# Cross-attention and feed-forward of a Flamingo block: attention one head at a time over all 16 units, each head one tile of 128 tokens, the feed-forward of a tile between later heads, SiLU from Tanh

## Chip, cores and metric

One NeuronCore of one Trainium2 chip runs the whole kernel; the metric is device time in microseconds of that core.
The kernel before takes 286.89 us (median of three runs, 286.7 to 287.58). In what follows PE is TensorE, DVE is VectorE, ACT is ScalarE, POOL is GpSimd, SP is SyncE, whose queue only starts DMAs, and PEld is PE's weight load.

## What is computed

```
x: (16 units, 64 rows, 256)   ctx: (16, 64, 256)
q = layernorm(x);  k = v = ctx;  8 heads of 8 rows each, both axes of the scores are the 256 columns
qk  = einsum('bhdq,bhdl->bhql', q, k) / sqrt(8)
ret = einsum('bhql,bhdl->bhdq', softmax(qk), v)
x   = x + tanh(g_xattn) * gamma * ret
h   = silu(Wg @ quant8(layernorm(x))) * (Wu @ quant8(...))      weights rounded to -1, 0, 1
x   = x + tanh(g_ffn) * (Wd @ quant8(rms_norm(h)))              inner size 1024, 1024 tokens in all
```

So there are 128 attention problems (16 units by 8 heads), each with scores of 256 by 256, and then a quantised feed-forward over 1024 tokens, which is 8 tiles of 128.

## The kernel before

**Exact scores from bf16.** q and k are each split into three bf16 parts. The parts go to DRAM (`scr_q`, `scr_k`, `parts_to_dram`, L203) and come back stacked over 72 partitions (`load_stack`, L222 for q, L225 for k), so that one bf16 product of 72 rows gives the score in nearly full precision. Partitions 96 and 97 hold the negated row maximum in two parts, which `score` adds to the product.

**Attention, unit by unit.** A unit's eight heads stand side by side in one stack buffer (`qs`, `ks`, four buffers, a buffer is 2048 columns). Work goes in batches of four heads, two batches to a unit. For each head: `score_for_max` (L871, two matmuls of 256 columns into one of two banks `mb`), the row maximum on DVE (L663), and after a whole unit a transpose (L910), a copy on ACT (L522, `cast_maxima`), the low part on DVE (L671, `cut_maxima`), and two DMAs that write the maxima to the stack's shift rows (`shift_rows`, L254, `qs<-mp`). Then `score` (L884), Exp on ACT over two heads at once (L506), and the value product (L899, eight matmuls per two heads). The maxima run LEAD = 5 batches, 20 heads, ahead of the scores; the transpose of a unit's maxima stands eight heads ahead of its first score. `next_stack` reloads a buffer once all scores of its unit are done. The loop is rolled: first and last four units by hand, `Fori(1, ITERS - 1)` between.

**Sums.** The value product also gives the denominators. ACT copies them out (L514), POOL's queue sends them to DRAM and fetches them by token (L378, L387, L390), DVE inverts (L680, L682), SP sends the inverses round by DRAM (`scr_i<-inv` L270, `invt<-scr_i` L282), and POOL multiplies and adds to x (L405, L408).

**Feed-forward, after all attention.** DVE computes the statistics and quantises x for four tiles and then twice for two (L720 to L753). Per tile: PE transposes x (L954), eight matmuls of 512 columns for gate and up (L965, into two pairs of banks `s`), Silu on ACT (L576), the product on DVE (L778), the square sum on ACT (L586), the norm weight on POOL (L446), the maximum on DVE (L783), a few 128x1 scale steps on DVE (L791 to L799), scaling on POOL (L453), rounding on ACT (L597), eight transposes (L973), their copy on DVE (L804), the down product (L980), and the result (L811), which SP stores. Sixteen matmuls of `keep_warm` (L1000) stand near the beginning.

## Time and profile before

| | |
|---|---|
| median of the runs | 286.89 us (286.7, 287.58, 286.89) |
| profiled execution, first to last instruction | 285.5 us |
| PE busy | 166.9 us (58%) |
| DVE busy | 176.3 us (62%) |
| ACT busy | 127.1 us (45%) |
| POOL busy | 106.7 us (37%) |
| mean granted clock of TensorE | 0.875 |
| moved by DMA | 27.45 MB, mean 96 GB/s |

The span is what the profile covers; the run's time adds what lies around it, and for the profiled execution only the span is given (the runs lie 1.2 to 2.1 us above it). A busy share says how much an engine did and not whether it set the pace: no engine reaches two thirds here, so the pace is set by waits, and the chain of waits names them. Three stretches matter: the preparation to about 70 us (first maxima at 31 us, first scores at 71 us), attention to about 208 us, and the feed-forward to the end.

### The profile page before, as it was taken

The page shows a single profiled execution, that of the slowest core. Times are in us where ns is not written, and L with a number is a line of the kernel's source. Part 1 is how long each engine was busy: PE and PEld are TensorE (multiplying, and loading weights), DVE is VectorE, ACT ScalarE, POOL GpSimd, SP SyncE. Part 2 cuts the span into 40 slices and gives each one's busy share as a digit, 9 for nine tenths or more (in the row PEclk, how much of TensorE's full clock was granted, in tenths as well). Part 3 has the DMA queues.
Part 4 walks back from the last instruction along what each step waited for, and adds up shares of the span by engine and source line. Part 5 has one row for each costly group of instructions (what it writes and reads, how often), then busy time and mean ns, then how long its engine had stood idle before and what let it go on. Part 6 is the DMA issues. An engine that isn't in the chain of part 4 may idle for free.

```text
span 285.5 us, 4321 instructions
## 1 busy us (share of the span) xinstructions
PE 166.9 (58%) x1262; PEld 82.6 (29%) x1266; DVE 176.3 (62%) x349; ACT 127.1 (45%) x176; POOL 106.7 (37%) x177
## 2 busy tenths in 40 slices
PE   0000323400976856956948938939995686658564
PEld 0000000100633423523523514514542233234342
DVE  7898323500763743753744834825989987988962
ACT  1424000000682861743833824815687247447840
POOL 5928000001020330330350520341657877937960
PEclk9999999999997996995995996986999579678955
DMA  6666311991521921121222222231212200000011
GB/s 186 207 198 211 123 71 79 239 227 78 176 96 79 269 100 80 63 94 79 88 100 82 71 101 94 68 101 70 69 40 72 60 2 22 1 19 23 32 37 39
DMA packets 15494, 27.45 MB, mean 96 GB/s; under 512 B 4558, under 2 KB 8782, under 8 KB 15478
## 3 DMA queue, kind: packets, MB, share of 16 engines
q1 hardware_dynamic: 13430, 23.96, 26.0%
q0 software_dynamic: 2048, 3.29, 3.7%
q8 instruction: 8, 0.13, 0.2%
q14 instruction: 8, 0.07, 0.1%
HBM read 19.53 MB, written 7.47 MB: 95 GB/s over the span
## 4 chain that ended last, share of the span: by engine, by line
PE 28%; DMA 26%; DVE 18%; SPq 10%; issue 8%; POOL 7%; ACT 1%; POOLq 0%; DVEq 0%; ACTq 0%
DMA ks<-scr_k 15%; PE mb L871 8%; PE s L884 7%; PE ob L899 7%; DMA qs<-mp 6%; DMA scr_i<-inv 4%; SPq L222 3%; DVE qf L647 3%; POOL rk L446 3%; SPq L239 3%; PE s L965 2%; POOL qf L453 2%; DMA scr_q<-qp 2%; DVE kf L732 2%; SPq L225 1%
## 5 line engine op out<-in xcount | busy, mean ns | idle before, releaser
L663 DVE TENSOR_REDUCE mx<-mb 128x2 f32<-128x512 f32 x128 | 83.7, 687 | 88.1 <-PE mb L871 87.1
L871 PE MATMUL mb<-ks,qs 128*128 128x256 bf16 x256 | 58.9, 322 | 78.9 <-DMA ks<-scr_k 71.4
L506 ACT ACTIVATE pr<-s 128x1024 f32<-128x1024 f32 x64 | 64.5, 1020 | 26.3 <-PE s L884 25.9
L884 PE MATMUL s<-qs,ks 128*128 128x256 bf16 x256 | 54.5, 304 | 12.1 <-DMA qs<-mp 12.0
L369 POOL COPY vw<-vt 128x32 f32<-128x32 f32 (+1 forms) x64 | 10.7, 214 | 126.7 <-PE ob L899 84.7
L871 PEld LDWEIGHTS mb<-ks,qs 128*128 128x128 bf16 x256 | 21.7, 108 | 113.5 <-issue 63.8
L899 PE MATMUL ob<-pr,vw 128*32 128x256 f32 x512 | 44.4, 422 | 1.5 <-ACT osb L514 0.7
L522 ACT ACTIVATE mp<-mtb 16x128 bf16<-16x128 f32 x16 | 4.3, 266 | 79.5 <-PE mtb L910 53.4
L884 PEld LDWEIGHTS s<-qs,ks 128*128 128x128 bf16 x256 | 26.3, 108 | 22.7 <-DMA qs<-mp 13.3
L965 PE MATMUL s<-wt,xt 128*128 128x512 bf16 x60 | 21.1, 504 | 11.3 <-DVE rq L778 6.5
L446 POOL TENSOR_TENSOR rk<-rq,lnw 128x1024 f32<-128x1024 f32 x8 | 18.8, 2348 | 5.1 <-DVE rq L778 5.1
L576 ACT ACTIVATE sg<-s,gsc 128x512 f32<-128x512 f32 x16 | 10.8, 683 | 18.4 <-PE s L965 18.4
L899 PEld LDWEIGHTS ob<-pr,vw 128*32 128x32 f32 x512 | 10.8, 113 | 17.7 <-issue 13.9
L980 PE MATMUL mb<-wt,ht 128*128 128x256 bf16 x64 | 11.0, 330 | 7.7 <-DVE ht L804 7.7
L378 POOL DMA_DIRECT2D scr_o<-osb x16 | 10.4, 648 | 9.3 <-ACT osb L514 6.2
L965 PEld LDWEIGHTS s<-wt,xt 128*128 128x128 bf16 x64 | 7.1, 119 | 21.9 <-issue 8.6
L597 ACT ACTIVATE yi<-qf 128x1024 bf16<-128x1024 f32 x8 | 8.4, 1055 | 6.2 <-POOL qf L453 6.0
L778 DVE TENSOR_TENSOR rq<-s,sg 128x512 f32<-128x512 f32 x16 | 10.3, 682 | 0.5 <-ACT sg L576 0.5
L387 POOL DMA_DIRECT2D num<-scr_o x16 | 9.9, 616 | 2.0 <-issue 1.7
L647 DVE TENSOR_SCALAR qf<-qf,mv,rs 128x256 f32<-128x256 f32 x8 | 9.4, 1232 | 1.8 <-POOL rs L341 1.8
L783 DVE TENSOR_REDUCE ym<-rk 128x1 f32<-128x1024 f32 x8 | 9.7, 1210 | 0.2 <-POOL rk L446 0.2
L980 PEld LDWEIGHTS mb<-wt,ht 128*128 128x128 bf16 x64 | 6.6, 114 | 10.9 <-DVE ht L804 9.4
(84 smaller groups left out, 205.2 us busy)
## 6 DMA issues: line engine op xcount, KB each, us to landing
qs<-scr_q SPq DMA_DIRECT2D x15, 288.0 KB
ks<-scr_k SPq DMA_DIRECT2D x15, 288.0 KB
scr_k<-kp SPq DMA_DIRECT2D x10, 256.0 KB, 2.9
scr_o<-osb POOLq DMA_DIRECT2D x16, 128.0 KB, 3.0
scr_q<-qp SPq DMA_DIRECT2D x6, 256.0 KB, 3.4
qf<-in_xh SPq DMA_DIRECT2D x2, 512.0 KB, 5.5
kf<-in_kh SPq DMA_DIRECT2D x2, 512.0 KB, 6.9
vt<-in_vt SPq DMA_DIRECT2D x1, 1024.0 KB, 27.8
```

What stands on the lines that cost most here:

```text
L369: nc.gpsimd.tensor_copy(dst, src).then_inc(v_filled, 1)
L378: pool.dma_start(scr_o[bass.ds(i * BUFS + k, 1)].rearrange("o p n -> (o p) n"), osb[:, k % 2, :]).then_inc(sums_out[k % 2], DMA)
L446: nc.gpsimd.tensor_tensor(y[:, par, :], z[:, par, :, :].rearrange("p a n -> p (a n)"), lnw[:, :], ALU.mult).then_inc(y_done, 1)
L506: nc.scalar.activation(pr[:, slot:slot + 2, :, :].rearrange("p h c n -> p h (c n)"), s2[pair][:, :, :], ACT.Exp, scale=float(DH) ** -0.5). ...
L576: nc.scalar.activation(sg[:, h, :], s2[h][:, 0, :], ACT.Silu, scale=gsc[:, bass.ds(t, 1)]).then_inc(silued, 1)
L647: nc.vector.tensor_scalar(cols, cols, mv[:, j, 0:1], rs[:, j:j + 1], ALU.subtract, ALU.mult).then_inc(normed, 1)
L663: nc.vector.tensor_reduce(mx[:, unit % 2, 2 * j:2 * j + 2], mb[h % 2][:, :].rearrange("p (c n) -> p c n", c=KC), axis=AX.X, op=ALU.max, ne ...
L871: mm = nc.tensor.matmul(mb[h % 2][:, c * COLS:(c + 1) * COLS], columns(qs, b, j, c), head(ks, b, j), start=True, stop=True)
L884: mm = nc.tensor.matmul(s2[pair][:, h % 2, c * COLS:(c + 1) * COLS], columns(ks, b, j, c), head(qs, b, j), start=True, stop=True)
L899: mm = nc.tensor.matmul(ob[32 * g:32 * g + 32, r, :], vw[:, r, c, 4 * a + g, :], pr[:, 4 * (b % 2) + g, c, :], start=(a == 0 and c == 0), ...
L965: mm = nc.tensor.matmul(s2[h][:, n, :], xt[:, c, :], w[:, c, h * 512:(h + 1) * 512], start=(c == 0), stop=(c == KC - 1))
L980: mm = nc.tensor.matmul(op_, ht[:, c, :], wdt[:, c, :], start=(c == 0), stop=(c == IC - 1))
```

## The change

The order of the work is new on every engine. Attention now runs head by head: head t of all 16 units is one stack (4096 columns, three buffers), and its 128 output rows (16 units by 8 rows) are exactly one tile of the feed-forward. The program is unrolled into 208 steps; step n is (T, p) with T = n // 16 and p = n % 16. In a step stand: the maximum product of problem n, the score of problem n - 14 (LAG), every fourth step the values of four problems, and at fixed p the feed-forward of tile T - 4 or T - 5. Scores go to a ring of three single banks that the transposed maxima share; Exp is now per head. The maxima of eight problems form a group (at both ends of the order of four), and its transpose stands five steps ahead of the group's first score. Attention ends in T = 8, the feed-forward in T = 12. Gate and up have one bank each (`gb`, `ub`), which the transposes and the down product use too.

Silu(x) comes from Tanh: ACT computes tanh(x/2), DVE adds 1 and multiplies by x, then by the up product (two DVE operations where one was). The 128x1 scale steps, the normalisation of x and the cutting of the weights move from DVE to POOL (more than a dozen small operations per tile, each waiting for the one before); the copy of `ht` and the last rounding of x move from DVE to ACT. POOL's DMAs of the sums move to SP. `keep_warm`, the zero rows and the separate load of x by token are gone. Preparation: head 0's parts are made and stored first, then the rest; the parts go out as runs of 512 bytes, and the loads of a stack have other outer dimensions.

The core of the diff:

```diff
...
@@ -20,23 +10,57 @@
...
-IC = INNER // P
-BUFS = 4
+KC, IC = COLS // P, INNER // P
+PER = UNITS
+TOTAL = TILES * PER
+SPAN = UNITS * COLS
...
 QMAX = 127.0
 ROUND = 1.5 * 2.0 ** 23
-SHIFT_ROW = 96
 TWO_ONES = 1.0 + 0x3F80 / 2.0 ** 23
-LEAD = 5
-ITERS = UNITS // BUFS
+KROWS = 9 * DH
+SROWS = KROWS + 2
 DMA = 16
-FREE = 2
-FREE1 = 1
-ANY = -99
+STACKS = 3
+VBUFS = 4
+
+LAG = 14
...
-            def load_stack(unit, k, lo, n_cols, arrived):
-
-                src = scr_q[bass.ds(unit, 1), :, :, lo:lo + n_cols].rearrange("o n d c -> (o n d) c")
-                sp.dma_start(qs[0:9 * DH, k, lo:lo + n_cols],
-                             bass.AP(src.tensor, src.offset, [[0, 3], [FREE_N, 3 * DH], [1, n_cols]])).then_inc(arrived, DMA)
-                src = scr_k[bass.ds(unit, 1), :, :, lo:lo + n_cols].rearrange("o n d c -> (o n d) c")
-                sp.dma_start(ks[0:9 * DH, k, lo:lo + n_cols],
-                             bass.AP(src.tensor, src.offset, [[DH * FREE_N, 3], [FREE_N, 3 * DH], [1, n_cols]])).then_inc(arrived, DMA)
-
-            parts_to_dram(parts, 0)
-            parts_to_dram(parts[:2], 1)
-            sp.wait_ge(q_clear, 1)
-            sp.wait_ge(k_clear, 1)
-            sp.wait_ge(parts_out[0], 8 * DMA)
...
-            def next_stack(i, k):
-
-                sp.wait_ge(scored, i * 16 + 4 * (k + 1))
-                sp.sem_inc(passed[3], 1)
-                sp.dma_start(qs[SHIFT_ROW:SHIFT_ROW + 2, k, :], zrow[:, :]).then_inc(stack_in[k], DMA)
-                load_stack(i * BUFS + (k + BUFS), k, 0, FREE_N, stack_in[k])
-
-            def shift_rows(i, k):
-
-                buf = k % BUFS
-                sp.wait_ge(max_cut, i * BUFS + (k + 1))
-                for n in range(2):
-                    row = qs[SHIFT_ROW + n:SHIFT_ROW + n + 1, buf, :].rearrange("o (h q) -> o h q", q=P)
-                    sp.dma_start(row, mp[:, n, :]).then_inc(shift_in[buf], DMA)
...
+            def load_stack(t, lo, hi, arrived):
+                src = scr_q[t].rearrange("a d u c -> (a d) (u c)")[:, lo:hi]
+                sp.dma_start(qs[0:KROWS, t % STACKS, lo:hi], bass.AP(src.tensor, src.offset, [
+                    [SPAN, 3 * DH], [0, 3], [1, hi - lo]])).then_inc(arrived, DMA)
+                for r in range(3):
+                    src = scr_k[t, r:r + 3].rearrange("a d u c -> (a d) (u c)")[:, lo:hi]
+                    sp.dma_start(ks[r:KROWS:3, t % STACKS, lo:hi], src).then_inc(arrived, DMA)
+
+            def wait_parts(t):
+                sp.wait_ge(q_out[t], DMA)
+                sp.wait_ge(k_out[t], 2 * DMA)
+
+            def next_stack(t):
+                wait_parts(t)
+                sp.wait_ge(k_ones, min(t, STACKS - 1) + 1)
+                if t >= STACKS:
+                    sp.wait_ge(scored, PER * (t - STACKS + 1))
+                load_stack(t, 0, SPAN, stack_in[t % STACKS])
...
+            for T in range(1, 13):
+                if 0 <= T - 2 < TILES:
+                    sums_to_dram(T - 2, 1)
+                if 1 < T + 1 < TILES:
+                    next_stack(T + 1)
+                if T < TILES + 1:
+                    shift_rows(2 * T if T < TILES else groups - 2)
+                if T == TILES:
+                    shift_rows(groups - 1)
+                if 0 <= T - 2 < TILES:
+                    sums_by_token(T - 2)
+                    inv_to_dram(T - 2)
+                if T < TILES:
+                    shift_rows(2 * T + 1)
+                if 0 <= T - 1 < TILES:
+                    sums_to_dram(T - 1, 0)
+                if 0 <= T - 2 < TILES:
+                    inv_by_token(T - 2)
+                if 0 <= T - 5 < TILES:
+                    store(T - 5)
             for par in range(2):
-                sp.wait_ge(o_out[par], (TILES // 2 + 1) * DMA)
-
+                sp.wait_ge(o_out[par], DMA * TILES // 2)
 
         @block.gpsimd
         def _(pool):
-            pool.sem_inc(att_done, FREE)
...
-            def silu(t, first):
-                for h in range(2):
-                    act.wait_ge(gu_done, t * 2 + (h + 1))
-                    if not first:
-                        act.wait_ge(z_done, t * 2 + (h - 1))
-                    act.sem_inc(passed[1], 1)
-                    nc.scalar.activation(sg[:, h, :], s2[h][:, 0, :], ACT.Silu,
-                                         scale=gsc[:, bass.ds(t, 1)]).then_inc(silued, 1)
-
-            def square(t, par, first):
-                act.wait_ge(z_done, t * 2 + 2)
...
+            def tanh_gate(t, h):
+
+                act.wait_ge(gu_done, 2 * t + h + 1)
+                act.wait_ge(a_scaled, t + 1)
+                if t >= 1:
+                    act.wait_ge(z_done, 2 * (t - 1) + h + 1)
+                nc.scalar.activation(th[:, h, :], gb[:, :], ACT.Tanh, scale=ghs[:, t:t + 1]).then_inc(tanh_done, 1)
+
...
+            def exp(m):
+
+                b = m // 4
+                if m % 4 == 0 and b >= 2:
+                    act.wait_ge(pv_done, b - 1)
+                act.wait_ge(scored, m + 1)
+                nc.scalar.activation(pr[:, b % 2, m % 4, :], score_slot(m)[:, :], ACT.Exp, scale=float(DH) ** -0.5).then_inc(exp_done, 1)
+
...
-            def gate_up(t, par, first):
-
-                for h in range(2):
-                    dve.wait_ge(silued, t * 2 + (h + 1))
-                    if not first and h == 0:
-                        dve.wait_ge(squared, t - 1)
-                        dve.wait_ge(y_done, t - 1)
-                    nc.vector.tensor_tensor(z[:, par, h, :], s2[h][:, 1, :], sg[:, h, :], ALU.mult).then_inc(z_done, 1)
-
-            def max_h(t, par):
+                nc.vector.tensor_scalar(wgh[:, :], wmean[:, 0:1], 0.5, None, ALU.mult).then_inc(w_stat, 1)
...
+            def gate_up(t, h):
+
+                dve.wait_ge(tanh_done, 2 * t + h + 1)
+                nc.vector.scalar_tensor_tensor(out=th[:, h, :], in0=th[:, h, :], scalar=1.0, in1=gb[:, :],
+                                               op0=ALU.add, op1=ALU.mult).then_inc(z_half, 1)
+                dve.wait_ge(z_half, 2 * t + h + 1)
+                if t >= 2 and h == 0:
+                    dve.wait_ge(squared, t - 1)
+                    dve.wait_ge(y_done, t - 1)
+                nc.vector.tensor_tensor(z[:, t % 2, h * 512:(h + 1) * 512], ub[:, :], th[:, h, :], ALU.mult).then_inc(z_done, 1)
+
+            def max_y(t):
...
+            for n in range(STEPS):
+                T, p = divmod(n, PER)
+                if n < TOTAL:
+                    reduce(n)
+                if n - 2 in TURN_AT:
+                    cut_maxima(TURN_AT[n - 2])
+                if T == 2 and p == 3:
+                    weigh_means()
+                if p == 2 and 0 <= T - 3 < TILES:
+                    mean_x(T - 3)
+                if p == 3 and 0 <= T - 3 < TILES:
+                    var_x(T - 3)
+                if p == 4 and 0 <= T - 4 < TILES:
+                    gate_up(T - 4, 0)
+                if p == 6 and 0 <= T - 3 < TILES:
+                    max_x(T - 3)
+                if p == 7 and 0 <= T - 4 < TILES:
+                    gate_up(T - 4, 1)
+                if p == 8 and 0 <= T - 2 < TILES:
+                    invert(T - 2)
+                if p == 12 and 0 <= T - 4 < TILES:
+                    max_y(T - 4)
+                if p == 13 and 0 <= T - 5 < TILES:
+                    result(T - 5)
 
         @block.tensor
         def _(pe):
-            pe.sem_inc(pv_done, FREE)
-            pe.sem_inc(h_turned, FREE1)
-            pe.sem_inc(down_done, FREE1)
-
...
+            def ring_free(who):
+
+                i = SLOT[who] - 3
+                if i >= 0:
+                    kind, at = RING[i]
+                    if kind == "score":
+                        pe.wait_ge(exp_done, at + 1)
+                    else:
+                        pe.wait_ge(max_cut, at + 1)
+
+            def score_for_max(n):
...
-            def keep_warm(count):
-
-                for n in range(count):
-                    nc.tensor.matmul(ob[:, :, :].rearrange("p r n -> p (r n)"), identb[:, :], wt[:, 0, 0:512], start=True, stop=True)
-
-            period(0, 0, 0, TILES)
-            keep_warm(16)
...
+            for n in range(STEPS):
+                T, p = divmod(n, PER)
+                if n < TOTAL:
+                    score_for_max(n)
+                if n in TURN_AT:
+                    turn_maxima(TURN_AT[n])
+                if 0 <= n - LAG < TOTAL:
+                    score(n - LAG)
+                b = (n - PV_LAG) // 4
+                if (n - PV_LAG) % 4 == 0 and 0 <= b < TOTAL // 4:
+                    values(b)
+                if T == 2 and p == 2:
+                    pe.wait_ge(consts, 3)
+                    sum_weights()
+                if p == 2 and 0 <= T - 4 < TILES:
+                    gate_up(T - 4, 0)
+                if p == 5 and 0 <= T - 4 < TILES:
+                    gate_up(T - 4, 1)
+                if p == 9 and 0 <= T - 5 < TILES:
+                    turn_h(T - 5)
+                if p == 11 and 0 <= T - 5 < TILES:
+                    down(T - 5)
+                if p == 12 and 0 <= T - 3 < TILES:
+                    turn_x(T - 3)
 
```

On SP's queue, in the rolled loop of the kernel before, one unit (`scored` counts scores done, `max_cut` the low parts of maxima):

```order
L245 DMA qs<-zrow 2x2048 [waits scored]
L222 ISA
L222 DMA qs<-scr_q 72x1x2048
L225 ISA
L225 DMA ks<-scr_k 72x1x2048
L251 REGISTER_ALU
L254 DMA qs<-mp 1x16x128 [waits max_cut]
L254 DMA qs<-mp 1x16x128
```

The same queue after the change, one whole T (16 heads) of the attention:

```order
L257 DMA scr_o<-osb 128x256 [waits o_copied]
L223 DMA qs<-scr_q 72x1x4096 [waits k_ones,scored,k_out4,q_out4]
L227 DMA ks<-scr_k 24x4096 x3
L249 DMA qs<-mp 1x16x128 [waits max_cut]
L249 DMA qs<-mp 1x16x128
L265 DMA den<-scr_o 128x1x32 [waits sums_out1]
L267 DMA num<-scr_o 128x1x256
L272 DMA scr_i<-inv 8x16x32 [waits inverted]
L249 DMA qs<-mp 1x16x128 [waits max_cut]
L249 DMA qs<-mp 1x16x128
L257 DMA scr_o<-osb 128x256 [waits o_copied]
L279 DMA invt<-scr_i 128x1x256 [waits inv_out1]
```

One reload now brings 16 heads instead of 8, as four DMAs instead of two; the shift rows of a group still stand behind the reload, and the sums' DMAs now stand in the same queue.

PE's queue after the change, p = 2 to p = 7 of a T with feed-forward (`sr_n` are the ring's banks, `gb` and `ub` gate and up):

```order
L810 MATMUL sr<-qs,ks 128x256 [waits max_cut]
L810 MATMUL sr<-qs,ks 128x256
L824 MATMUL ob<-pr,vw 32x256 [waits o_copied,v_filled,exp_done]
L824 MATMUL ob<-pr,vw 32x256 x7
...
L858 MATMUL gb<-wt,xt 128x512 [waits z_done]
L858 MATMUL gb<-wt,xt 128x512
L858 MATMUL ub<-wt,xt 128x512 x2
L791 MATMUL mb<-ks,qs 128x256 [waits max_taken]
L791 MATMUL mb<-ks,qs 128x256
L810 MATMUL sr<-qs,ks 128x256 [waits exp_done,shift_in0]
```

The second score behind a transpose now waits for `max_cut`, because the ring has three banks; the second half of gate and up waits for DVE's product of the first (`z_done`); and the next maximum products stand behind both.

## Rows read from the trace of the kernel before

**Rows 1.** The page: busy tenths of DVE and of the DMA engines, in 40 slices.
```profile
DVE  7898323500763743753744834825989987988962
...
DMA  6666311991521921121222222231212200000011
```
**Rows 2.** Chain of waits: start us, us, what.
```profile
36.23 0.71 SPq L225
...
42.61 7.57 SPq L239
...
50.23 2.57 SPq L254
...
52.84 17.89 DMA qs<-mp
...
120.58 10.03 DMA ks<-scr_k
...
148.32 10.21 DMA scr_i<-inv
```
**Rows 3.** Waits: engine, line, releaser: us in total, times, longest us.
```profile
DVE mx L663 <- PE mb L871: 87.1, 60, 12.3
```
**Rows 4.** Stretches: length, busy PE, PEld, DVE, ACT, POOL, clock, DMA share, GB/s.
```profile
50.00:62.00 12.00, 4.14 (x14) 0.87 (x13) 4.64 (x8) 0.00 (x0) 0.00 (x0) 1.00 0.97 247
...
126.50:139.50 13.00, 8.77 (x66) 4.32 (x67) 5.46 (x9) 5.10 (x7) 2.10 (x7) 0.74 0.24 91
138.00:144.00 6.00, 5.98 (x65) 3.40 (x63) 5.17 (x12) 5.12 (x8) 2.16 (x7) 1.00 0.21 71
```
**Rows 5.** Shift DMAs (L254) issued at 182.83 and 183.48: us from issue to landing.
```profile
DMA to landing us min/median/max: 2.2/5.5/8.9
```
**Rows 6.** Chain, PE in attention: half clock at 134, full clock at 138.
```profile
132.83 1.01 PE ob L899 x8
...
134.38 0.43 PE s L884 x2
...
138.89 0.57 PE ob L899 x8
139.46 0.33 PE mb L871 x2
139.79 0.22 PE s L884 x2
```
**Rows 7.** Groups by line: out<-in, shapes, count | busy us, mean ns | idle before.
```profile
L663 DVE TENSOR_REDUCE mx<-mb 128x2 f32<-128x512 f32 x128 | 83.7, 687 | 88.1 <-PE mb L871 87.1
L506 ACT ACTIVATE pr<-s 128x1024 f32<-128x1024 f32 x64 | 64.5, 1020 | 26.3 <-PE s L884 25.9
L576 ACT ACTIVATE sg<-s,gsc 128x512 f32<-128x512 f32 x16 | 10.8, 683 | 18.4 <-PE s L965 18.4
L446 POOL TENSOR_TENSOR rk<-rq,lnw 128x1024 f32<-128x1024 f32 x8 | 18.8, 2348 | 5.1 <-DVE rq L778 5.1
L439 POOL TENSOR_TENSOR rh<-vh,mhalf 128x1 f32<-128x1 f32 x8 | 4.4, 552 | 5.1 <-ACT vh L591 4.3 <-POOL qf L453 0.8
L453 POOL TENSOR_SCALAR qf<-rk,sh 128x1024 f32<-128x1024 f32 x8 | 9.0, 1121 | 2.0 <-DVE sh L799 1.9 <-issue 0.2
L527 ACT ACTIVATE wt<-wf 128x2048 bf16<-128x2048 f32 x3 | 5.7, 1912 | 0.0
L783 DVE TENSOR_REDUCE ym<-rk 128x1 f32<-128x1024 f32 x8 | 9.7, 1210 | 0.2 <-POOL rk L446 0.2
```
**Rows 8.** Timeline of the feed-forward: start us, us, engine, line, operation.
```profile
246.64 3.59 PE L965 MATMUL s<-wt,xt 128*128 128x512 bf16 x8 [1.14 <-DVE rq L778]
...
261.14 1.89 PE L965 MATMUL s<-wt,xt 128*128 128x512 bf16 x8
...
275.35 1.03 PE L973 MATMUL mtb<-identb,yi 128*128 128x128 bf16 x8 [0.49 <-ACT yi L597]
277.17 1.89 PE L980 MATMUL mb<-wt,ht 128*128 128x256 bf16 x8 [0.79 <-DVE ht L804]
```

1180 lines of the change are left out of this document (518 added, 662 removed).

## The prediction

> **What bounds the kernel now.** I read the page first, then the chain of waits, then single stretches. No engine is full, and DVE, the busiest, has two holes, near 60 us and in a saw-tooth through attention [rows 1]. The waits say whose fault that is: DVE stands 87.1 us for the maximum products on PE [rows 3], and the chain goes from those to `ks<-scr_k`, a stack reload of 10.0 us that comes once per unit [rows 2]. In a stretch where almost only such reloads run, the DMA share is 0.21 at 71 GB/s, while the loads of 50 to 62 us reach 0.97 and 247 GB/s [rows 4]. 0.21 of 16 engines is three: the reload of a unit (288 KB for q and 288 KB for k) sits on three engines, whose outer dimension in `load_stack` is 3. Eight heads then cost 10 us, 16 heads 20.5 us, whatever the engines do.
>
> The Trainium skill, DMA: Bandwidth & Descriptors, "Why a DMA increments its semaphore by 16 and not by 1", gives the rule: a DMA uses the largest number of engines up to 16 that divides the outermost dimension of both sides. By that rule the old reload has 3 engines, and the trace agrees (0.21); the new ones, 24 rows against 72 and 24 against 24, would have 12.
>
> Where the reload does not hold it, PE does: in full clock two heads take 0.57 for the values and 0.33 and three times 0.22 for the products, with gaps 1.55 us, where DVE needs 2 times 0.69 [rows 6, 7]. In half clock the same is 2.84 us (value product 1.01, each pair 0.43) [rows 6]. The preparation ends at 70.7 us, when the first shift rows land after 17.9 us behind stacks and weights [rows 2]. The feed-forward needs 77 us from 208 us on.
>
> **Preparation.** Head 0 alone is loaded, split and stored, so I put its stack in place at 22 us instead of 31 (0.25 MB instead of 2 MB in front of the first statistics, casts of 256 columns, a 3 us round to DRAM, four issues of 0.7 us [rows 2]). 14 maxima follow at 0.66 us each, and PE then stands at score 0. What it waits for is a long queue: SP issues 14 DMAs of parts (9 us, to 32), then `vt` (landed near 39), POOL fills the values and only then sets the one rows of the other stack buffers (42), SP reloads stack 1 (to 45), and the first shift rows land at 49.5. Score 4 at n = 18 needs the second group, whose shift rows stand behind 3 MB of weights: at 247 GB/s [rows 4] that is 12.7 us from 47 on, so with landing **62 us**. The step that is late before (17.9 us behind the same weights) is thus late again; the gain is 9 us, with 18 maxima done instead of 20.
>
> **A T without feed-forward.** The reload of 1.18 MB takes 4.2 us if 12 engines each keep the rate of rows 4's three (24 GB/s), 6.4 us at the 15.4 GB/s that each of 16 has at 247 GB/s; both are below a T, so the 20.5 us bound goes. What is late next is the shift row. It stands behind the reload in every ring: before, one issued right behind a reload lands after 8.9 us, otherwise after 2.2 [rows 5]. Before, it has eight heads of time, now five. I count from the start of a T: copy of the sums and its DMA to 2.2, four reload issues to 5.3, shift issue to 6.5, landing at 8.7. PE reaches p = 6 at 5.5 (DVE's six maxima 4.1, the low part 0.27, and 1.4 in which DVE has no bank because PE waits for the low part at p = 3 and then does the values). Wait 3.2 us. From p = 6 to p = 13 the same takes 7.2; the second group is not behind a reload and costs 0.8; two steps and values 2.1. Sum 5.5 + 3.2 + 7.2 + 0.8 + 2.1 = 18.8, say **19 us**, for T = 3. T = 1 and T = 2 also carry the weights on ACT: 16 Exp of 0.60 (half of 1.02 and a fixed part), three passes of 2.1 [rows 7], 0.9 of copies, 17 us, in segments that wait for the same shift rows: 15.5 us from n = 18 to the end of T = 1 and **20.5 us** for T = 2.
>
> **A T with feed-forward (four of them).** DVE: 16 x 0.687 = 11.0, low parts 0.54, four operations of 512 columns 2.7 (the two of the SiLU cost 1.4 more than before), `ym` 1.2, statistics, `am`, inverse and result 1.8: 17.3 us. ACT: Exp 9.6, tanh 1.4, square 1.25, `yi` 1.06, `ht` 1.05, copies 2.0: 16.3 us. PE in full clock: 12.4 for attention, 1.9 for gate and up [rows 8], 0.6, 1.1 and 0.3 for the rest: 16.3 us. POOL: 2.35 + 1.12 + 0.55 for each of five powers [rows 7], ten small operations at 0.2 to 0.4, which no row shows alone and which I take at 0.3 with their waits, two additions of 0.9: 13 us. None of these is the period, because they wait for each other: tanh of half 0 stands behind the score that waits for the low part, gate and up of half 1 behind DVE's product of half 0, tanh of half 1 behind the score that waits for the shift row (landed at 8.7, needed at 8.6, so here nearly free), and the down product with the values at p = 11 leaves DVE without a bank for 2.8 us. Followed step by step in full clock: 8.7 to p = 6, 13.1 from there, **21.8 us**. In half clock PE needs twice as long. A stretch of 13 us behind such a wait has a granted clock of 0.74 [rows 4], which is 6.8 us at 1.2 GHz and the rest at 2.4; I take 1.2 us a T for it: **23 us**, and 92 us for the four.
>
> **The rest.** T = 8 has the last scores and no maxima; ACT sets the pace with 15.5 us, I take 17. From T = 9 the feed-forward is alone with one pair of banks: gate and up 1.0, tanh 0.75, two DVE operations 1.35, the same again, eight transposes 0.9, `ht` 1.05, down 1.9 [rows 8], next transposes and copy 0.8: 10.1 with 0.1 for each hand-over, and POOL's own chain of scales is 11: 12 us each for T = 9 and 10. From T = 11: product of half 1 at 6.5, POOL's weight 2.35, maximum 1.2, scales and scaling 2.75, `yi` 1.05, transposes 1.03, copy 1.05, down 1.89, result 0.5, store 2: **21 us**, 45 us in all.
>
> **Sum**: 62 + 15.5 + 20.5 + 19 + 92 + 17 + 45 = 271 us, against the profiled span of 285.5. The median stands 1.4 above that span, so the time is **272.4 us**. In short: 9 us from the start, attention with half of the feed-forward in it ends about 18 us later than attention before, and after it 45 to 62 us are left instead of 77.
>
> **Rivals.**
> *Tight pipeline.* The waits I added (low part, values without a bank, shift row) overlap better, and a T costs what its fullest engine does plus a little: 17, 17 and 15 for T = 1 to 3, 19 for the next four. 62 + 14 + 17 + 15 + 76 + 15 + 44 + 1.4 = 244. For it: before, DVE idles only 0.26 in 1.55 us in full clock. Against: the order has more waits in a line than before. Chance 0.22.
> *Half clock holds (slower).* The order has two or three short stops of PE per T where before there is one long one per 20 us. If half clock covers most of it, attention costs 16 heads x 1.42 = 22.7 us of PE [rows 6], plus 3.59 for gate and up [rows 8] and 2 for the rest: 28.3 us in T = 4 to 7, 22 in T = 2 and 3. 62 + 17 + 44 + 113 + 18 + 46 + 1.4 = 301. It decides from about 26.5 us per T on. For it: the clock of 0.74 behind one stop [rows 4]. The Trainium skill, TensorE: Matmul & The Clock Gate, "HAM oscillation", says that waits for DMA put the clock back again and again, which speaks for this. Chance 0.15.
> *Reload still on three engines (slower).* 1.18 MB at 71 GB/s are 16.6 us, the shift row behind it lands at 19 us of a T, which becomes 29 us or more: over 330 us. Chance 0.04.
> *Small operations on POOL set the pace (slower).* At 0.5 us each instead of 0.3, and with DVE's and the DMAs' hand-overs, POOL needs 16 us, and the way of the inverse round by DRAM (10.2 us before, behind a reload [rows 2]) pushes `yi` onto ACT's queue ahead of the Exp: 26.5 us a T and 15 in the end, 294. Chance 0.09.
>
> **How the numbers follow.** The forecast has 0.50. Its own range, 258 to 286, comes from the POOL and `vt` chain (5 us either way), the 1.2 us of clock (0 to 3 per T), and 1 us per T of overlap. Taking in the tight pipeline's 244 to about half and both slower cases up to 297 leaves 2 in 10 outside: 247 to 297. A measurement of this kernel tells 0.3%, 0.9 us, from no change. Faster: nearly all of 0.50, and 0.22: 0.71. The same: 0.04. Slower: 0.25.
>
> **What would show it.** Right: first maximum product at 22 us, a stop of PE from 31 to 50 and another to 62, DMA share above 0.5 in a reload, a wait of PE for `qs<-mp` of 3 us per T early on, maxima of T = 4 starting near 117 and its period near 23 us, PE's last attention product near 225. Wrong: reloads at a share of 0.2, granted clock below 0.75 on average in attention, or POOL as the releaser of DVE's `am` and ACT's `yi` in each T.

## The result, and the profile after

| | before | after |
|---|---|---|
| median | 287.54 us (286.7 to 288.25, 6 runs) | 311.73 us (304.93 to 316.44, 6 runs) |
| ratio | | 1.066, 95% interval 1.058 to 1.074 |
| profiled span | 285.5 us | 314.5 us |
| PE, DVE, ACT, POOL busy | 166.9, 176.3, 127.1, 106.7 us | 191.6, 142.3, 138.1, 150.2 us |
| mean granted clock | 0.875 | 0.751 |

The change makes the kernel slower by 6.6%; the forecast was 272.4 us (247 to 297), faster. The changed kernel scatters by 11 us where the kernel before scatters by 1.5 (and by up to 5 in the later sets). Its profiled execution is the longest of the six. The ratio comes from the two shortest runs, which span 302.8 and 305.3 us at a clock of 0.787 and 0.779, and single stretches of this profile can be some microseconds longer than in those.

The page: rows of the 40 slices, and two of the groups.

```profile
PE   0045004378877956866897888488877675344433
DVE  3775202254433553474554745555584433334320
PEclk9999999996557576796555677857897999555555
DMA  3679739920240060151106013401101112000000
...
L675 DVE TENSOR_REDUCE mx<-mb 128x2 f32<-128x512 f32 x128 | 85.4, 684 | 112.4 <-PE mb L791 110.8
L810 PE MATMUL sr<-qs,ks 74*128 74x256 bf16 x256 | 63.7, 344 | 54.4 <-DMA qs<-mp 36.2 <-DVE mp L682 17.1 <-ACT pr L522 1.2
```

Against [rows 1, 3] three things stand out. DVE did the same 128 maxima at the same price, and waited for PE not 87.1 but 110.8 us. The DMA row now has short peaks with nothing between them. And the clock row lies at 5 to 7 in most slices of attention; its mean is 0.751, where before it was 0.875.

One caution on that row. It shows 1.00 up to its first recorded change, at 65.7 us here and near 74 us before, although the matmuls up to there have the durations of half clock (a score pair takes 0.61 to 0.64 us, and 0.38 to 0.39 in full clock). So the means are too high in both kernels, and where a clock matters, the duration of a matmul has to confirm it.

The reload itself did what was forecast. Windows of the kernel after, in a reload and over the blocks T = 2 to T = 8 and the rest; columns as in [rows 4].

```profile
113.00:118.00 5.00, 2.88 (x22) 1.42 (x14) 2.40 (x4) 1.39 (x3) 2.23 (x4) 0.54 0.76 207
...
82.80:109.90 27.10, 21.55 (x132) 10.48 (x131) 11.63 (x23) 15.63 (x23) 13.98 (x10) 0.56 0.23 66
109.90:134.60 24.70, 17.52 (x136) 8.93 (x135) 11.69 (x23) 10.41 (x23) 7.01 (x14) 0.72 0.26 72
134.60:162.70 28.10, 21.84 (x140) 10.77 (x139) 15.73 (x28) 12.45 (x26) 11.16 (x21) 0.67 0.23 63
162.70:192.40 29.70, 25.51 (x160) 12.68 (x159) 16.02 (x29) 14.32 (x29) 13.88 (x25) 0.62 0.24 65
192.40:222.60 30.20, 22.79 (x156) 12.01 (x155) 15.93 (x29) 14.29 (x28) 12.15 (x23) 0.72 0.25 63
222.60:247.30 24.70, 17.90 (x157) 9.52 (x156) 15.04 (x29) 14.44 (x31) 12.99 (x24) 0.93 0.10 30
247.30:262.80 15.50, 11.22 (x117) 5.67 (x115) 6.02 (x12) 12.28 (x24) 8.87 (x16) 1.00 0.17 46
262.80:314.50 51.70, 21.05 (x91) 9.91 (x88) 15.20 (x24) 16.91 (x24) 30.95 (x56) 0.54 0.06 19
```

A share of 0.76 in the reload is twelve engines of sixteen, where [rows 4] had 0.21, three. Its data moves from about 112 to 119 us, somewhat longer than the forecast's 4.2 to 6.4 us. The forecast's rule for the number of engines (the Trainium skill, DMA: Bandwidth & Descriptors, "Why a DMA increments its semaphore by 16 and not by 1") therefore agrees with the trace.

Then the blocks. Each T = 4 to 7 was to take 23 us; they take 28.1, 29.7, 30.2 and 24.7. In each of them PE is busy for most of the time (21.8, 25.5, 22.8, 17.9 us) at a clock of 0.67, 0.62, 0.72 and 0.93, for work that in full clock is 16 us. The one with the least PE time is T = 7, the block in which no stack is reloaded.

Where PE stops, its timeline shows at T = 3, which begins at 109.9 (start, duration, and in brackets the idle time ahead and what ended it).

```profile
112.17 0.39 PE L810 MATMUL sr<-qs,ks 74*128 74x256 bf16 x2 [1.46 <-DVE mp L682]
112.49 1.14 PE L824 MATMUL ob<-pr,vw 128*32 128x256 f32 x16
113.56 0.61 PE L791 MATMUL mb<-ks,qs 72*128 72x256 bf16 x2
...
120.13 0.61 PE L810 MATMUL sr<-qs,ks 74*128 74x256 bf16 x2 [4.26 <-DMA qs<-mp]
120.53 0.63 PE L791 MATMUL mb<-ks,qs 72*128 72x256 bf16 x2
120.96 0.64 PE L810 MATMUL sr<-qs,ks 74*128 74x256 bf16 x2
121.52 1.94 PE L824 MATMUL ob<-pr,vw 128*32 128x256 f32 x16
...
126.90 0.54 PE L810 MATMUL sr<-qs,ks 74*128 74x256 bf16 x2 [0.98 <-DVE mp L682]
127.37 1.93 PE L824 MATMUL ob<-pr,vw 128*32 128x256 f32 x16
...
132.06 1.07 PE L824 MATMUL ob<-pr,vw 128*32 128x256 f32 x16
```

There are three stops of 1.46, 4.26 and 0.98 us, and between and behind them the same sixteen value matmuls take 1.94 us in half clock and 1.07 in full. SP issued those shift rows at 113.56, behind the four transfers of the reload:

```profile
109.90 0.32 SPq L257 DMA_DIRECT2D scr_o<-osb  x1
110.40 0.84 SPq L223 DMA_DIRECT2D qs<-scr_q  x1
111.28 2.23 SPq L227 DMA_DIRECT2D ks<-scr_k  x3
113.56 1.19 SPq L249 DMA_DIRECT2D qs<-mp  x2
114.80 0.65 SPq L265 DMA_DIRECT2D den<-scr_o  x1
```

They were usable at 120.1, 10.2 us into the block (forecast: 8.7). The DMA engines are busy with the reload until about 119 us: the share is 0.57 from 118 to 118.5 us and 0.07 from 119 to 119.5.

### The profile page after: what moved, and what is told of

Same layout as the page of the kernel before. It is cut to its first block, busy times and chain, and to the rows that moved or that the text cites. A ratio compares the mean times of both kernels' runs of the same rounds, so it can differ in the third digit from the quotient of the medians.

```text
span 314.5 us, 3742 instructions
## 1 busy us (share of the span) xinstructions
PE 191.6 (61%) x1252; PEld 94.5 (30%) x1252; DVE 142.3 (45%) x257; ACT 138.1 (44%) x247; POOL 150.2 (48%) x236
## 4 chain that ended last, share of the span: by engine, by line
PE 34%; POOL 16%; DMA 16%; DVE 13%; SPq 9%; issue 5%; ACT 5%; POOLq 0%; ACTq 0%; DVEq 0%
PE ob L824 12%; DMA qs<-mp 11%; PE sr L810 8%; PE mb L791 7%; DVE mx L675 6%; SPq L227 3%; POOL qf L373 3%; PE ub L876 2%; DMA xh<-in_xh 2%; SPq L253 2%; PE gb L858 2%; DMA invt<-scr_i 2%; DVE wf L720 2%; PE ub L858 2%; POOL scr_q L385 2%
## 5 line engine op out<-in xcount | busy, mean ns | idle before, releaser
L675 DVE TENSOR_REDUCE mx<-mb 128x2 f32<-128x512 f32 x128 | 85.4, 684 | 112.4 <-PE mb L791 110.8
L522 ACT ACTIVATE pr<-sr 128x512 f32<-128x512 f32 x128 | 75.3, 594 | 119.2 <-PE sr L810 118.7
L810 PE MATMUL sr<-qs,ks 74*128 74x256 bf16 x256 | 63.7, 344 | 54.4 <-DMA qs<-mp 36.2
L791 PE MATMUL mb<-ks,qs 72*128 72x256 bf16 x256 | 66.9, 357 | 28.0 <-DMA ks<-scr_k 19.2
L810 PEld LDWEIGHTS sr<-qs,ks 74*128 74x128 bf16 x256 | 28.1, 120 | 72.8 <-DMA qs<-mp 38.9
L791 PEld LDWEIGHTS mb<-ks,qs 72*128 72x128 bf16 x256 | 25.9, 121 | 62.9 <-issue 37.3
L446 POOL TENSOR_TENSOR wf<-wf,lnw 128x1024 f32<-128x1024 f32 x8 | 18.8, 2350 | 12.1 <-DVE wf L726 8.1
L858 PE MATMUL gb<-wt,xt 128*128 128x512 bf16 x32 | 12.2, 471 | 15.2 <-DVE wf L726 13.0
L876 PE MATMUL ub<-wt,ht 128*128 128x256 bf16 x64 | 13.9, 392 | 5.5 <-ACT ht L590 5.5
L720 DVE SCALAR_TENSOR_TENSOR wf<-wf,gb 128x512 f32<-128x512 f32 x16 | 10.9, 683 | 12.3 <-ACT wf L569 12.1
L867 PE MATMUL gb<-identb,yi 128*128 128x128 bf16 x64 | 7.0, 275 | 14.9 <-DVE wf L726 11.1
L858 PE MATMUL ub<-wt,xt 128*128 128x512 bf16 x32 | 12.3, 474 | 0.0
```

Source lines behind the costliest of these rows:

```text
L446: nc.gpsimd.tensor_tensor(y[:, t % 2, :], z[:, t % 2, :], lnw[:, :], ALU.mult).then_inc(y_done, 1)
L522: nc.scalar.activation(pr[:, b % 2, m % 4, :], score_slot(m)[:, :], ACT.Exp, scale=float(DH) ** -0.5).then_inc(exp_done, 1)
L675: nc.vector.tensor_reduce(mx[:, h % 2, 2 * at:2 * at + 2], mb[n % 2][:, :].rearrange("p (c n) -> p c n", c=KC), axis=AX.X, op=ALU.max, neg ...
L720: nc.vector.scalar_tensor_tensor(out=th[:, h, :], in0=th[:, h, :], scalar=1.0, in1=gb[:, :], op0=ALU.add, op1=ALU.mult).then_inc(z_half, 1)
L791: mm = nc.tensor.matmul(mb[n % 2][:, c * COLS:(c + 1) * COLS], qs[0:KROWS, t % STACKS, at:at + P], ks[0:KROWS, t % STACKS, u * COLS:(u + 1 ...
L810: mm = nc.tensor.matmul(score_slot(m)[:, c * COLS:(c + 1) * COLS], ks[0:SROWS, t % STACKS, at:at + P], qs[0:SROWS, t % STACKS, u * COLS:(u ...
```

## Experiments

Theory at the start: the new order stops PE two or three times a block, at the low part and at the shift rows behind the reload, and the rest of the loss is what these stops bring with them. Rivals: half clock by itself, the second operation of the SiLU on DVE, the value product that leaves DVE without a bank, and POOL. Each set of runs had the kernel before beside it; its median moved by less than 2 us between sets. Where a ratio to it was formed, the ratio decides; medians of the changed kernel carry its scatter of 11 us.

**One part alone: the reload on twelve engines in the kernel before.**

```diff
-  bass.AP(src.tensor, src.offset, [[0, 3], [FREE_N, 3 * DH], [1, n_cols]])
+  bass.AP(src.tensor, src.offset, [[FREE_N, 3 * DH], [0, 3], [1, n_cols]])
...
-  sp.dma_start(ks[0:9 * DH, k, ...], AP([[DH * FREE_N, 3], [FREE_N, 3 * DH], ...]))
+  for r in range(3):
+      sp.dma_start(ks[r:9 * DH:3, k, ...], scr_k[unit, r:r + 3, ...])
```

> The kernel before with one part of the change alone: a stack is reloaded with 24 as outer dimension (one DMA for q, three for k) instead of 3. Theory (reload bound): attention before is held by the three DMA engines at 10 us a unit; with more engines a reload takes 4 to 6 us, 16 heads cost 13 to 15 us of PE instead of 20.5, and the run is 25 to 40 us shorter, near 250 to 262 us. Rival (the wait only moves): shift rows and issues on the queue (two more DMAs of 0.7 us per unit) take its place, gain under 10 us. If the reload still has three engines: DMA share stays 0.2 and the time stays at 287 us.

230.39 us (229.09 to 230.88), ratio 0.806 (0.799 to 0.812), 56 us less. Its page:

```profile
PE   0000033739999599979977999999389458487573
DVE  6998743738887588768866897889998979979942
PEclk9999999999999999999999999999857997889855
DMA  5857654699638823443533443212110000001101
```

The last row maximum starts at 149 us instead of 207 and the last value product at 161 instead of 218. PE is at 9 tenths in most slices of attention, the clock stays full in them, and the 60 us from 80 to 140 hold 68 of the maxima, which is 14 us for 16 heads. So the old bound was worth 56 us, more than the 25 to 40 expected, and the kernel before with that one edit is some 80 us faster than the changed kernel, which has the edit too (75 by the ratios).

**The reload undone in the changed kernel.**

```diff
-  [SPAN, 3 * DH], [0, 3], [1, hi - lo]])
+  [0, 3], [SPAN, 3 * DH], [1, hi - lo]])
...
-  for r in range(3):
-      src = scr_k[t, r:r + 3] ...
-      sp.dma_start(ks[r:KROWS:3, ...], src)
+  sp.dma_start(ks[0:KROWS, ...], AP([DH * SPAN, 3], [SPAN, 3 * DH], ...))
```

> The changed kernel with its reload undone: the rows of a stack are fetched with an outer dimension of 3 as before, on three DMA engines. Theory (the reload's engines are the one good part of the change; in the kernel before they were worth 56 us): a reload takes 10 us again, each stop for the shift rows behind it grows by 4 to 6 us, 325 to 345 us. Rival (the waits for the low part and the shift rows hide a long reload, since a whole stack lies between its issue and its use): 308 to 318 us.

380.15 us (379.76 to 381.84), ratio 1.325 (1.316 to 1.334): 68 us more than the changed kernel, above the range of either theory. A window behind the issue of a reload, and the block T = 4:

```profile
156.00:170.00 14.00, 1.43 (x7) 0.70 (x5) 2.16 (x4) 1.19 (x2) 2.28 (x7) 0.50 0.21 83
...
183.70:217.60 33.90, 18.09 (x141) 9.04 (x140) 15.37 (x28) 12.30 (x27) 11.13 (x21) 0.75 0.15 52
```

The share is 0.21 again, and PE is all but idle in the first window: the shift rows behind the long reload stop it (109.9 us in 8 stops by the waits). T = 3 to 6 take 32 to 34 us, T = 7, without a reload, 24.2. So the reload's engines were not one small part. What the rest of the change costs can be read twice: 92 us on three engines (380 against 288), and some 80 us on twelve (312 against 230).

**The shift rows ahead of the reload**, in the changed kernel.

```diff
+  if T < TILES + 1:
+      shift_rows(2 * T if T < TILES else groups - 2)
   if 1 < T + 1 < TILES:
       next_stack(T + 1)
-  if T < TILES + 1:
-      shift_rows(2 * T if T < TILES else groups - 2)
```

> The changed kernel with the shift rows of group 2T issued before the reload of stack T+1, and not behind it. Theory of my prediction: PE waits about 3 us per T for them in T = 2 and 3 and less than 1 us later; so 5 to 9 us less in all. Theory of the clock: the stop of 3 us is one of those that put the clock back, and the T after it get shorter as well, 10 to 15 us less. Rival: the waits for the low part and for banks are the ones that count, under 3 us.

298.57 us (297.86 to 300.44), ratio 1.045 (1.036 to 1.054): 13.2 us less in the median, 6 us by the ratios (1.045 against 1.066). The first number lies in the range of the theory of the clock, the second in that of the prediction's theory, so the times don't decide between them. The blocks speak for the clock: T = 4 to 7 take 100.2 us instead of 112.7, with PE idle for 24.8 us where it was 24.7, and busy for 75.4 where it was 88.0. The wait of PE for `qs<-mp` went from 36.2 us in 7 stops to 23.0 in 2, and those two are in the preparation.

**Fillers in the stops, on the changed kernel.** Matmuls into the free bank, behind the last maximum: 4 at p = 3 and 11, 6 at p = 5, 6 and 14 of T = 3 to 7, 8 to 40 in the end.

> The changed kernel with filler matmuls of 256 columns (results overwritten) where PE stands: in T = 3 to 7 four before a score that waits for the low part, six before one that waits for shift rows and before the second half of gate and up; after attention 8 to 12 before each feed-forward step. Theory of the clock: half clock is what makes a T of feed-forward 28 us and not 22; with the stops filled the granted clock in T = 3 to 8 goes from 0.7 to above 0.9, those T shrink by 4 to 6 us each, the tail from T = 9 by 5 us, in all 20 to 30 us less, 280 us. Rival (waits in a line set the period): clock rises but the time stays within 5 us, or gets longer by the fillers (about 0.1 us each, some 3 us per T).

303.79 us (302.82 to 307.34), ratio 1.066 (1.056 to 1.076). The clock rose from 0.751 to 0.898, and the result is about the changed kernel's shortest run. T = 5 and 6 in full clock:

```profile
161.10:185.50 24.40, 19.89 (x186) 11.74 (x185) 15.81 (x29) 14.20 (x29) 10.18 (x20) 1.00 0.29 78
185.50:210.80 25.30, 19.66 (x184) 11.53 (x183) 15.71 (x29) 14.02 (x29) 12.83 (x24) 1.00 0.28 76
```

They take 5 us less than in the changed kernel's profile, T = 4 (clock 0.70) and T = 7 nothing less. But these fillers don't make the kernel fast: PE is busy for 19.9 and 19.7 us in these two blocks where its own work is 16, so some 4 us of each are now fillers. The scatter is 4.5 us; whether the clock makes the 11 us of the changed kernel isn't shown, for of its six runs the one with the highest mean clock, 0.797, took 313.3 us.

**Values in two pieces, on the changed kernel**, so that DVE has a bank sooner: 8 matmuls one step earlier, 8 one step later.

> The changed kernel with the value products of four heads in two pieces of eight matmuls, two steps apart (one step earlier and one later), as the kernel before had them. Theory of coupling (DVE is left without a bank for the 1.9 us that the values take in half clock, more with the down product behind it): 1 to 2 us less per T, 8 to 14 us in all. Theory of the clock alone: no stop of PE goes away, within 3 us. Rival: the copy of the sums on ACT at the start of a T now comes one step later, slower by 1 to 4 us.

316.94 us (315.02 to 323.1), ratio 1.104 (1.093 to 1.115). A miss: slower, and by more than the rival allowed. DVE still waits 107.4 us for the maximum products (110.8 before), so the split doesn't take that wait away. The clock row has a mean of 0.842 here, but up to 144 us it holds no recorded change and shows 1.00, and the matmuls say otherwise (eight value matmuls inside that stretch and in full clock later):

```profile
112.87 1.08 PE L825 MATMUL ob<-pr,vw 128*32 128x256 f32 x8
...
173.90 0.64 PE L825 MATMUL ob<-pr,vw 128*32 128x256 f32 x8
```

PE ran at half clock through T = 2 and T = 3, which take 27.0 and 27.7 us, and is busy for 206.3 us in all, against 191.6. So this run doesn't speak against half clock as a cause. Why it stayed there for so long isn't shown.

**Without the product of x in the SiLU, on the changed kernel.** This kernel leaves out the operation that forms (1 + tanh) times x; the gate is tanh alone, 16 DVE operations fewer.

> The changed kernel with one of the two DVE operations of the SiLU left out (the product of 1 + tanh with x: the gate is then tanh alone), 16 operations of 0.68 us. Theory (they stand in the line z of half 0, gate and up of half 1, tanh, z of half 1, also in the tail): 1.4 us less per T in nine T, 10 to 14 us. Rival (they are covered by waits for PE): under 4 us.

307.64 us (306.18 to 310.3), ratio 1.070 (1.062 to 1.079). No effect by the ratio: the extra operation of the SiLU costs nothing that shows here.

**The cut of the maxima one step earlier**, on top of the shift rows first.

```diff
-  if n - 1 in TURN_AT:
-      cast_maxima(TURN_AT[n - 1])
+  if n in TURN_AT:
+      cast_maxima(TURN_AT[n])
...
-  if n - 2 in TURN_AT:
-      cut_maxima(TURN_AT[n - 2])
+  if n - 1 in TURN_AT:
+      cut_maxima(TURN_AT[n - 1])
```

> The changed kernel with the shift rows ahead of the reload (as in a1_shift_first) and, besides, the maxima of a group cast one step earlier on ACT (before that step's Exp) and their low part one step earlier on DVE. Theory (waits in a line set the period): PE waits 1 to 1.5 us for the low part twice a T and the shift rows leave one step earlier; 1.5 to 2.5 us less per T, 10 to 18 us below a1_shift_first's 298.6. Rival (clock): the stops stay, only shorter, so the clock stays near 0.8 and the gain is under 5 us.

281.99 us (281.38 to 287.38), ratio 0.982 (0.972 to 0.991): 16.6 us less than with the shift rows first alone, by moving two small operations, as the theory had it. The clock is in it as well (mean 0.835 against 0.800): T = 4 to 7 are 11.1 us shorter, and PE's busy time makes 5.4 of that, its idle time 5.7. PE's wait for the low part fell from 15.5 to 3.5 us. Since the shift rows went first, another wait has come up in the list of waits (10.4 us in 4 stops there, not in the changed kernel's list), and here it is the next to go (us in all, times, the longest):

```profile
DVE inv L690 <- DMA den<-scr_o: 14.0, 5, 4.9
```

DVE's inverse waits for the sums, whose fetch is queued on SP behind the reload, as the shift rows were.

**The same cut, with the shift rows left behind the reload.**

> The changed kernel with the early cast and cut of the maxima alone; the shift rows stay behind the reload, where they waited 36.2 us in 7 stops. Theory (waits in a line on PE's queue: each takes away its own time whatever the others do): 293 to 300 us, as much less than 311.7 as the same edit gave behind the other order (16.6 us). Rival (the shift rows behind the reload end the second stop of each block whenever the cut comes, so half of the gain is hidden): 301 to 308 us.

303.65 us (295.51 to 308.27), 8.1 us less than the changed kernel; no ratio was formed, so the medians have to do. T = 4 to 6 fall from 28.1, 29.7, 30.2 to 27.3, 26.6, 27.2 us, T = 7, which has no reload to wait for, from 24.7 to 20.4 at full clock. By the median that is the rival, but the shortest run, 295.51 us, lies in the theory's range, so the times alone don't decide. The waits do: those of PE for the low part fell from 17.1 to 4.6 us, and those for shift rows rose from 36.2 to 41.9. Of 12.5 us won at the low part, 5.7 are waited for at the shift rows instead.

**Fillers on top of the shift rows first**, fewer than above.

> a1_shift_first with fillers in the stops of attention only, from T = 1 on (three before a score that waits for the low part, four before one that waits for shift rows and before the second half of gate and up). Theory of the clock: granted clock in attention above 0.95, T = 2 to 7 shorter by 2 to 3 us each, 12 to 18 us below 298.6. Rival (waits in a line): the T shrink by less than 1 us each.

302.19 us (299.61 to 304.98), ratio 1.049 (1.037 to 1.061), against 1.045 without them. No gain, but no test of the clock either: its mean rose only from 0.800 to 0.822, and T = 4 to 7 lie at 0.74 to 0.93, where above 0.95 was expected.

**A longer lag**, the scores 18 instead of 14 behind the maxima, on the changed kernel, with the shift rows first and the sums later to suit.

> The changed kernel with LAG 18 instead of 14, so that a group's maxima are turned nine steps ahead of its first score and not five, shift rows ahead of the reload, and the steps that hang on the sums four steps later. Theory (lead too short): no wait of PE for shift rows is left in T = 1 to 7, 3 to 4 us less per T than in the changed kernel; 285 to 293 us. Rival: the later sums hold up the feed-forward of the next T, or the waits for the low part and the banks take over: 298 us as in a1_shift_first, or more.

293.94 us (291.27 to 301.37), ratio 1.017 (1.007 to 1.027). The shift rows cost PE 3.0 us in one stop, but the low part, which stands at a fixed distance from its transpose, still 16.7 in 14, and the preparation has a second wait for a stack, 17 us. Lag cures the transfer in the blocks, not the cut.

**The sums' fetch ahead of the reload**, on top of the early cut.

```diff
+  if 0 <= T - 2 < TILES:
+      sums_by_token(T - 2)
   if 1 < T + 1 < TILES:
       next_stack(T + 1)
```

> The version with the stack's shift rows ahead of the reload and the early cut (281.99 us), with the fetch of the softmax sums issued ahead of the next stack's reload on SP too. Theory (the sums' fetch stood behind the reload, DVE waited 14.0 us in 5 stops for it and PE behind DVE): DVE's wait for den falls below 3 us, T=3 to T=7 are 1 to 3 us shorter each, 270 to 276 us. Rival (the reload, issued later, now comes late for the next stack, or PE was waiting for something else at the same time): 280 to 284 us, with a wait of PE for the stack in its place.

269.9 us (267.12 to 274.12; before in the same set 288.01), 12.1 us less; no ratio was formed, but all its runs lie below all those without the edit. The wait for `den` is gone from the list of waits. Its blocks T = 3 to T = 8 and the rest:

```profile
95.60:114.80 19.20, 15.47 (x132) 7.77 (x131) 11.44 (x23) 10.26 (x24) 7.45 (x16) 0.84 0.34 92
114.80:136.70 21.90, 18.18 (x143) 9.71 (x143) 15.14 (x28) 12.63 (x28) 9.71 (x18) 0.83 0.32 81
136.70:156.40 19.70, 16.06 (x157) 9.32 (x157) 15.43 (x29) 14.03 (x29) 12.75 (x23) 1.00 0.36 97
156.40:177.40 21.00, 17.61 (x158) 9.82 (x157) 15.55 (x29) 14.15 (x29) 13.07 (x25) 0.92 0.34 91
177.40:198.00 20.60, 15.91 (x154) 8.97 (x154) 14.60 (x28) 14.22 (x31) 12.63 (x23) 1.00 0.12 35
198.00:214.20 16.20, 12.35 (x114) 6.26 (x115) 6.54 (x13) 12.21 (x24) 11.71 (x22) 0.89 0.15 44
214.20:265.50 51.30, 20.71 (x90) 9.89 (x89) 15.20 (x24) 16.93 (x24) 30.11 (x54) 0.54 0.07 19
```

T = 4 to 7 now take 83.2 us instead of 112.7. PE's busy time in them fell from 88.0 to 67.8 us, for the same matmuls, and its idle time from 24.7 to 15.4. So two thirds of what the three edits gave in these blocks is the clock, which came back by itself when the stops went. That isn't only the long profile of the changed kernel: the kernel without the product of x, profiled in 308.3 us and otherwise with the same matmuls, takes 109.1 us for T = 4 to 7 with PE busy for 86.7. The reload, now issued 3.7 to 5.2 us into a block instead of 0.5, is not late.

**Fillers on this version.**

> The fastest version of the changed kernel (269.9 us, mean clock 0.853) with filler matmuls in the stops of T=3 to T=7 and of the tail. Theory (with the waits gone TensorE's own work ends the blocks, so the clock counts: 86 us at half clock): mean clock over 0.92 and 260 to 266 us. Rival (the blocks are still chains through ACT and DVE, and the fillers fill time that comes back as nothing, as in the changed kernel itself): 268 to 274 us.

273.15 us (269.63 to 274.11), ratio 0.954 (0.949 to 0.958), clock 0.958. The clock is where the theory put it, the time is the rival's. T = 5 and 6 take 23.5 and 23.2 us with PE busy 20.7 and 20.5, where without fillers it is 16.1 and 17.6: they hold PE by more than the clock gives. The experiment doesn't tell what a full clock would be worth for free.

**The scale steps back on DVE for all tiles**, five of six small operations ahead of each hidden row's quantization.

> The same version, with five of the six 128x1 scale steps ahead of each hidden row's quantization moved from GpSimd back to VectorE, the inverse root computed on GpSimd right after the weighing. Theory (the last four tiles are a chain through GpSimd, some 12 us a tile, of which these small steps are 1.9 us of work and more in handovers): the tail of about 51 us is 5 to 10 us shorter, so 5 to 10 us below the version above. Rival (the tail is a chain of handovers whoever computes the steps, or VectorE's new waits hold its maxima in T=4 to T=7): within 2 us of it or slower.

278.63 us (275.21 to 279.42), ratio 0.971 (0.964 to 0.977), 8.7 us slower. T = 9 to the end takes 48.7 us instead of 51.3, but T = 4 to 7 take 98.1 instead of 83.2. Of these 14.9 us, 10.5 are PE's busy time, at a clock of 0.81 where it was 0.93, and DVE waits 28.3 us for the maximum products where it was 19.7. The list of waits has none of DVE for POOL's scales in these blocks, so that the new steps hold the maxima, as the rival says, isn't shown directly.

**The same for the last four tiles alone.**

> The same fastest version with the small scale steps on VectorE for the last four tiles alone. Theory (the tail is a chain through GpSimd and these steps are in it, while VectorE has nothing else to do there): 3 to 6 us less, 264 to 267 us, T=1 to T=7 unchanged. Rival (the tail's length is set by the handovers): 269 to 272 us.

264.99 us (259.84 to 275.58, 6 runs), ratio 0.924 (0.919 to 0.929). The end falls to 47.4 us, and T = 6 to 8 are unchanged to 0.2 us. Ahead of T = 8 the two kernels do the same, and yet T = 3 begins 3.5 us earlier and is 2.3 us shorter at a higher clock (0.90 for 0.84), T = 4 is 1.0 us shorter, and T = 5 took 22.5 us at a clock of 0.88 where it took 19.7 at 1.00. Blocks that differ like that are the likely reason why these runs lie 16 us apart. This is the fastest form of the changed order that I found, and 35 us slower than the kernel before with the reload edit.

**The preparation of the fastest kernel reordered**: in the kernel before with its reload on twelve engines, the first shift rows after two stacks, the value table and the third stack behind them, the weights last.

> The kernel before with its reload on twelve engines (230.39 us), and in the prologue the first stack's shift rows issued after two stacks instead of after three and the value table, the value weights after the second stack's shift rows. Theory (the first scores at 50 us and the stop after them wait for transfers in the order of issue): 3 to 5 us less, 225 to 227.5 us. Rival (what ends the stop is the transform's own chain): within 1 us of 230.4, or slower because the value table is late.

232.38 us (229.49 to 234.84), ratio 0.802 (0.795 to 0.810), against 0.806. In time that is the rival: no gain that these runs tell. But the first stop does follow the order of issue: the shift rows are issued at 42.2 instead of 45.2 us, and the first score starts at 48.1 instead of 50.2, with no wait for them. What takes the gain away is a new wait, 6.2 us at 61 to 67 us, for a stack whose reload was issued at 56 us, now right behind the 3 MB of weights.

## Why the prediction was wrong

The sum by its own terms, with the profiled span of 314.5 us, and in the last column the version without the three waits:

| term | forecast | after | without the waits |
|---|---|---|---|
| n = 18 resumes | 62 | 59.9 | |
| T = 1, rest | 15.5 | 22.9 | |
| T = 2 | 20.5 | 27.1 | |
| T = 3 begins | 98 | 109.9 | 95.6 |
| T = 3 | 19 | 24.7 | 19.2 |
| T = 4 to 7 | 92 | 112.7 | 83.2 |
| T = 8 | 17 | 15.5 | 16.2 |
| T = 9 to the end | 45 | 51.7 | 51.3 |
| span | 271 | 314.5 | 265.5 |

*The bound of before: right.* It was three engines (share 0.21), and it was worth more than the 25 to 40 us that I expected of the edit alone: 56 us.

*The preparation: right*, within 3 us at each mark (first maximum product 19.2 for 22, first score 51.7 for 49.5, n = 18 at 59.9 for 62), with the two stops of PE where they were put.

*The reload: right in its engines*, share 0.76, and below a block's length. It takes about 7 us and not 4.2 to 6.4, and the shift rows behind it are usable 10.2 us into the block and not 8.7. (The forecast read [rows 5] as 8.9 us behind a reload and 2.2 otherwise; both shift DMAs of that row stand behind the same reload.)

*The stops in a block: about right in size.* PE idles 24.7 us in T = 4 to 7, 6.2 a block; forecast was 21.8 less 16.3, which is 5.5. The shift rows behind the reload stop PE for 4.3 us in T = 3 (forecast 3.2), and 2.7 and 2.9 in two of the four blocks where I had them "nearly free".

*The clock: wrong, and this is the step that failed.* "I take 1.2 us a T for it: 23 us." PE was busy 88.0 us in the four blocks where full clock needs 16 to 16.3 each, so it cost about 5.8 us a block: some 18 of the 20.7 us that these blocks were too long. T = 2 and 3 (27.1 us at 0.56, 24.7 at 0.72) were too long by 12 more. I had read the clock behind one stop in 20 us [rows 4] and applied it once a block; and even that row, 6.8 us at half clock, is up to 3.4 us of PE's work, for which I took 1.2 without a reason. The forecast's own sign of being wrong, a clock below 0.75 in attention, is there: 0.73 from T = 2 to T = 8, and 0.66 up to T = 6.

The number of stops in a block doesn't give its clock, though. T = 5 has the lowest, 0.62, with waits of PE of 4.1 us in all and none above 1.3, and T = 7 has 0.93 with waits of 6.8 us. T = 5 inherits its clock: it fell at 144 us, behind 4 us in which PE was busy for 1.3, with the wait for shift rows in them, and rose only at 178. T = 7 begins in full clock and loses it once, for 3.5 us. Other falls (at 182 and 189 us) lasted 3.5 us each; what makes one last 3.5 and another 34 isn't shown. With half clock PE is also the busiest engine (25.5 of 29.7 us in T = 5, DVE 16.0), so most of what it adds lengthens the block. The rival *Half clock holds* had 28.3 us for T = 4 to 7; the trace has 28.2. It named this very mechanism, but that the numbers meet is luck: it had PE busy for all of 28.3 us, where PE is busy for 22.0 on average and idle for 6.2. Its chance of 0.15 was too small, and its 22 us for T = 2 and 3 too (27.1 and 24.7). T = 3, 4 and 6, in which PE waits for a DMA, lie at 0.72, 0.67 and 0.72; T = 5, in which it waits for none, at 0.62. The rule behind the rival (the Trainium skill, TensorE: Matmul & The Clock Gate, "HAM oscillation": waits for DMA put the clock back again and again) agrees with the fall in T = 4, and says nothing of a block like T = 5. How large the term was in the shorter runs isn't on record.

*The end: too short by 6.7 us.* I took POOL's chain at 11 us and 12 for a tile. By its timeline POOL goes from one inverse root of the hidden row to the next in 14.7 us (262.53 to 277.20), of which 11.8 are work:

```profile
262.18 0.27 POOL L451 TENSOR_SCALAR vh<-ss,us 128x1 f32<-128x1 f32 x1
262.53 0.57 POOL L452 TENSOR_TENSOR rh<-vh,mhalf 128x1 f32<-128x1 f32 x1
263.18 0.19 POOL L453 TENSOR_TENSOR fh<-rh,hsc 128x1 f32<-128x1 f32 x1
...
271.98 2.35 POOL L446 TENSOR_TENSOR wf<-wf,lnw 128x1024 f32<-128x1024 f32 x1
275.23 0.72 POOL L413 TENSOR_TENSOR num<-num,invt 128x256 f32<-128x256 f32 x1 [0.90 <-DMA invt<-scr_i]
```

The work is about what the forecast's terms add up to, which is 11.0 us (for a block it gives 13, which its terms don't add up to). What it left out are two waits, 0.54 us for DVE and 0.90 for the inverse's way round by DRAM, and about 0.1 us between each operation and the next, 1.5 in all. Moving these steps for the last tiles gave 3.9 us of the end, so POOL is part of it; full clock there gave 2. What makes up the rest of the end wasn't settled.

*What the change can be worth.* Without the three waits the span is 265.5 us against the forecast's 271, but that is two errors that offset each other: T = 4 to 7 take 8.8 us less than forecast, the end 6.3 more. And the same reload edit in the old order gives 230 us, so I had compared with the wrong thing as well: from T = 2 on the new order never reaches the old one's 14 us for 16 heads, and putting the feed-forward between the heads doesn't pay for that. In the 230 us kernel PE is at full clock in attention, and 76.5 us are left for the feed-forward of eight tiles behind the last maxima at 151 us; in the best form of the new order four tiles alone take 47.4. The 35 us between them I can't divide further.
